# Out-degrees summed by TensorE from the finished rows of counts, in place of a histogram of sources; the capacity check looks at in-degrees alone

## What is computed

```
src = randint(0, 3125)                          # 50000 of them, uniform
dst = int32(3125 * uniform() ** 2.0)            # 50000, skewed to low numbers
order = argsort(dst, stable); src, dst = src[order], dst[order]
deg  = segment_sum(ones, row=src)               # out-degree, layer 0
w    = rsqrt(deg)[src] * rsqrt(deg)[dst]        # where deg > 0
h    = segment_sum(w * x[dst], src) @ W + b     # layer 0
mean = segment_sum(h[src], dst) / max(in_deg,1) # the three mean layers
```

## Time and profile before

| what | value |
|---|---|
| median of 3 runs | 3809.99 us (3808.7 to 3810.3) |
| profiled execution | 3814.58 us, of which span 3812.8 us |
| mean granted clock of TensorE | 0.889 of full |
| DVE busy over the span | 1841.9 us (48%) |
| count_packed, from its first instruction to the first of the stage behind count_pairs | 81.70 to 541.20 us |

### The profile page before, as it was taken

One profiled execution on the slowest core, in us unless ns is written; L12 is line 12 of the kernel. 1 busy time (PEld: TensorE's weight loads), 2 busy tenths in 40 slices (PEclk: granted clock), 3 DMA queues, 4 the chain that ended last, 5 costly groups with the idle time before them and its releaser, 6 DMA issues. The chain is left out here.

```text
span 3812.8 us, 46850 instructions
## 1 busy us (share of the span) xinstructions
PE 2943.8 (77%) x13253; PEld 2097.5 (55%) x13317; DVE 1841.9 (48%) x4590; ACT 875.8 (23%) x1237; POOL 1276.3 (33%) x929
## 2 busy tenths in 40 slices
PE   1777759774666666699999969999998999655565
PEld 1345537643555544466666658989894444344443
DVE  5999852355888887533233323434344221322223
ACT  0135644220100101022222224444441222000000
POOL 2000000007777740177667720000000000477776
PEclk9999979886677678899999989999999999778777
DMA  2046768314444421212222127666861444433334
GB/s 60 18 172 221 270 238 276 113 55 146 129 135 132 128 59 42 78 59 80 80 80 72 68 96 258 199 212 196 276 193 67 142 144 138 124 105 105 105 105 123
DMA packets 325254, 504.89 MB, mean 132 GB/s; under 512 B 27225, under 2 KB 238877, under 8 KB 317005
## 3 DMA queue, kind: packets, MB, share of 16 engines
q1 hardware_dynamic: 284477, 391.28, 30.5%
q0 software_dynamic: 40672, 112.31, 10.6%
HBM read 351.56 MB, written 152.75 MB: 132 GB/s over the span
## 5 line engine op out<-in xcount | busy, mean ns | idle before, releaser
L1791 POOL DMA_INDIRECT e7got<-rel_d,rel_i x416 | 394.6, 948 | 1139.9 <-POOLq L2699 1013.4
L1911 POOL DMA_INDIRECT a_got<-feat_d,src_i x416 | 404.1, 971 | 409.5 <-POOLq L2240 283.0
L1827 PE MATMUL e7sums<-e7got,e7hot 128*128 128x256 f32 x832 | 289.6, 508 | 197.0 <-DMA e7got<-rel_d,rel_i 166.4
L1425 PE MATMUL s_aggs<-s_blk_r,high 128*128 128x512 f32 (+1 forms) x1050 | 400.8, 382 | 20.7 <-DVE low L1544 20.5
L1425 PE MATMUL s_aggs<-s_blk_r,low 128*128 128x512 f32 (+1 forms) x1050 | 389.1, 371 | 0.0
L2740 PE MATMUL q_prods<-w,q_xt 128*128 128x512 f32 x800 | 352.8, 599 | 13.4 <-ACT q_xt L2760 13.4
L1827 PEld LDWEIGHTS e7sums<-e7got,e7hot 128*128 128x128 f32 x832 | 203.0, 255 | 280.4 <-issue 243.2
L1643 POOL TENSOR_SCALAR g_absent<-g_pairs 128x3200 bf16<-128x3200 f32 x25 | 274.8, 10992 | 171.4 <-DMA g_pairs<-pairs_d 171.3
L1690 PE MATMUL g_sums<-value,g_turned 128*128 128x257 f32 x1250 | 299.0, 383 | 8.6 <-ACT g_turned L1754 8.6
L1668 PE MATMUL g_scores<-key_t,g_q 128*128 128x512 f32 (+1 forms) x700 | 280.6, 556 | 19.9 <-DMA g_q<-query_d 13.3
L1799 DVE TENSOR_SCALAR e7hot<-iota,dloc,weight 128x128 f32<-128x128 f32 x416 | 115.7, 364 | 356.6 <-PE e7sums L1827 348.1
(11 more groups left out here) (422 smaller groups left out, 4469.7 us busy)
## 6 DMA issues: line engine op xcount, KB each, us to landing
s_blk<-turned_d SPq DMA_DIRECT2D x60, 1280.0 KB, 5.9
rel_d<-q_rows SPq DMA_DIRECT2D x25, 2048.0 KB, 7.5
s_blk<-turned_d SPq DMA_DIRECT2D x45, 960.0 KB, 5.1
pairs_d<-u_rows SPq DMA_DIRECT2D x25, 1600.0 KB, 8.1
turned_d<-u_line SPq DMA_DIRECT2D x25, 1600.0 KB, 7.1
g_pairs<-pairs_d SPq DMA_DIRECT2D x25, 1600.0 KB, 6.8
t_blk<-pairs_d SPq DMA_DIRECT2D x20, 1280.0 KB, 10.0
t_blk<-pairs_d SPq DMA_DIRECT2D x15, 960.0 KB, 5.1
```

The lines of the kernel that those rows point to most:

```text
L1425: last = pe.matmul(aggs[:, idx % 2, half, 0:w], feats[l][part][:, a, half * P:(half + 1) * P], blk_r[:, q % RINGS, a % GA, 0:w], start=a = ...
L1791: pool.indirect_dma_start(got[:, j % U, :], None, table, bass.IndirectOffsetOnAxis(ap=index[:, j:j + 1], axis=0)).then_inc(arrived[j % U / ...
L1827: return pe.matmul(sums[:, 0:D], hot[:, u, :], got[:, u, :], start=False, stop=False)
L1911: pool.indirect_dma_start(got[:, n % 2, s, :], None, table, bass.IndirectOffsetOnAxis(ap=k.src_i[:, j:j + 1], axis=0)).then_inc(arrived[n ...
```

## The change

The marks and tallies in count_packed go, with hist and its two reductions. TensorE now sums the columns of rows itself. For each of the seven groups of a turn it first multiplies the group (w up to 512 columns of rows, as float32r) by marks[:, g, :], a 128x7 matrix with ones in column g, and accumulates into bank sums, whose row g then holds the out-degrees of group g. The transposes become products with a float32r identity. After the last turn, given gets the 7 x 512 sums, four transposes stand them upright, and two copies bring them to k.deg_src. The check takes **the largest in-degree alone** and compares it with 255.5; the out-degree and the minimum are gone. count_pairs is not edited. The diff, cut to its core (declarations of the names left out):

```diff
...
@@ -750,7 +751,7 @@
                       allow_small_or_imprecise_dtypes=True).then_inc(ready, 1)
             pool.memset(zero[:], 0.0).then_inc(ready, 1)
             pool.memset(hot_s[:, :, THIRD:W], 1.0).then_inc(ready, 1)
-            pool.memset(rows[:], 0.0).then_inc(ready, 1)
+            pool.memset(rows[:].bitcast(F32), 0.0).then_inc(cleared, 1)
 
         @block.vector
         def _(dve):
@@ -761,14 +762,12 @@
             step(dve.scalar_tensor_tensor(column[:], third[:], float(-THIRD), column[:], ALU.mult, ALU.add))
             step(dve.tensor_scalar(value[:], second[:], 255.0, 1.0, ALU.mult, ALU.add))
             step(dve.scalar_tensor_tensor(value[:], third[:], 65280.0, value[:], ALU.mult, ALU.add))
-            dve.wait_ge(ready, 4)
-
-            def marks(i, b):
-                dve.wait_ge(tallied, i + 1)
-                dve.tensor_tensor(marked[:, b, :, 0:P], k.iota_b[0:EP, :].unsqueeze(1).broadcast_to([EP, 4, P]),
-                                  cols(k.slo, i * 4, 4).unsqueeze(2).broadcast_to([EP, 4, P]), ALU.is_equal).then_inc(hot, 1)
-                dve.tensor_tensor(marked[:, b, :, P:P + T], k.iota_b[0:EP, 0:T].unsqueeze(1).broadcast_to([EP, 4, T]),
-                                  cols(k.shi, i * 4, 4).unsqueeze(2).broadcast_to([EP, 4, T]), ALU.is_equal).then_inc(hot, 1)
+            step(dve.tensor_copy(ident_r[:], k.ident[:]))
+            step(dve.tensor_copy(marks[:].rearrange("p g m -> p (g m)"), k.zero[:, 0:1].broadcast_to([P, FLIPS * FLIPS])))
+            step(dve.tensor_copy(marks[:].rearrange("p g m -> p (g m)")[:, 0:FLIPS * FLIPS:FLIPS + 1],
+                                 k.ones[:, 0:FLIPS]))
+            dve.sem_inc(marked, 1)
+            dve.wait_ge(ready, 3)
 
             def take_apart(t):
                 dve.wait_ge(copied, t * COPIES + 2 * COPIES)
@@ -789,10 +788,8 @@
             def eight(i, closing):
                 for u in range(8):
                     j = i * 8 + u
-                    if u % 4 == 0:
-                        if closing:
-                            closings((i * 2 + u // 4 - LOOK))
-                        marks(2 * i + u // 4, u // 4)
+                    if u % 4 == 0 and closing:
+                        closings((i * 2 + u // 4 - LOOK))
                     dve.wait_ge(used, j + 1)
                     dve.tensor_scalar(hot_d[:, u, :], k.iota_b[:], cols(k.dloc, j, 1), None, ALU.is_equal).then_inc(made, 1)
                     dve.tensor_scalar(hot_s[:, u, 0:THIRD], places[:], cols(column, j, 1), cols(value, j, 1),
@@ -804,23 +801,25 @@
             for group in range(S // 4 - LOOK, S // 4):
                 closings(group)
             take_apart(T - 1)
-            dve.wait_ge(final, 1)
-            step(dve.tensor_copy(k.deg_src[:], hist[:, 0:T]))
-            step(dve.tensor_reduce(largest[:, 0:1], k.deg_dst[:], AX.X, ALU.max))
-            step(dve.tensor_reduce(largest[:, 1:2], k.deg_src[:], AX.X, ALU.max))
+
+            step(dve.tensor_reduce(largest[:], k.deg_dst[:], AX.X, ALU.max))
             dve.sem_inc(reduced, 1)
             dve.wait_ge(laid, 1)
-            step(dve.tensor_reduce(flag[:, 0:1], hist[0:1, P:2 * P], AX.X, ALU.max))
-            step(dve.tensor_reduce(flag[:, 1:2], hist[0:1, 2 * P:3 * P], AX.X, ALU.max))
-            step(dve.tensor_tensor(flag[:, 0:1], flag[:, 0:1], flag[:, 1:2], ALU.min))
-            step(dve.tensor_scalar(flag[:, 0:1], flag[:, 0:1], 255.5, None, ALU.is_gt))
-            step(dve.tensor_copy(k.heavy[:], flag[:, 0:1]))
+            step(dve.tensor_reduce(flag[:], counts[0:1, 0, 0:P], AX.X, ALU.max))
+            step(dve.tensor_scalar(flag[:], flag[:], 255.5, None, ALU.is_gt))
+            step(dve.tensor_copy(k.heavy[:], flag[:]))
+            dve.wait_ge(final, 1)
+            step(dve.tensor_copy(given[:], sums[0:FLIPS, :]))
+            dve.sem_inc(given_in, 1)
+            dve.wait_ge(upright, 1)
+            by_group = counts[:, 1, 0:4 * FLIPS].rearrange("p (a g) -> p g a", a=4)
+            step(dve.tensor_copy(k.deg_src[:, 0:4 * (FLIPS - 1)].rearrange("p (g a) -> p g a", a=4), by_group[:, 0:FLIPS - 1, :]))
+            step(dve.tensor_copy(k.deg_src[:, 4 * (FLIPS - 1):T], by_group[:, FLIPS - 1, 0:T - 4 * (FLIPS - 1)]))
 
         @block.tensor
         def _(pe):
             pe.sem_inc(used, RING)
-            pe.sem_inc(tallied, 2)
-            pe.wait_ge(ready, 4)
+            pe.wait_ge(ready, 3)
 
             def zeros(b):
 
@@ -842,24 +841,21 @@
 
             for b in range(BANKS):
                 zeros(b)
-            pe.matmul(hist[:, 0:T], zero[0:EP, 0:P], zero[0:EP, 0:T], start=True, stop=False)
+            pe.matmul(sums[0:FLIPS, :], zero[:, 0:FLIPS], zero[:, 0:512], start=True, stop=False)
+            pe.wait_ge(marked, 1)
 
 
             def flip(closing, g):
                 pe.wait_ge(lined, closing * FLIPS + flip_room(g))
                 pe.sem_inc(k.passed, 1)
+                w = min(4, T - 4 * g) * P
+                pe.matmul(sums[0:FLIPS, 0:w], marks[:, g, :], rows[:, 4 * g * P:4 * g * P + w], start=False, stop=False)
                 for a in range(4 * g, min(T, 4 * g + 4)):
-                    last = pe.transpose(flips[:, g % 4, (a % 4) * P:(a % 4 + 1) * P], rows[:, a * P:(a + 1) * P], k.ident[:])
+                    last = pe.matmul(flips[:, g % 4, (a % 4) * P:(a % 4 + 1) * P], rows[:, a * P:(a + 1) * P], ident_r[:],
+                                     start=True, stop=True)
                 last.then_inc(flipped, 1)
 
-            def tally(i, b):
-                pe.wait_ge(hot, 2 * i + 2)
-                for u in range(4):
-                    last = pe.matmul(hist[:, 0:T], marked[:, b, u, 0:P], marked[:, b, u, P:P + T], start=False, stop=False)
-                last.then_inc(tallied, 1)
-
             def four(i, b):
-                tally(i, b)
                 word = load_word(pe, k, i)
                 with pe.If((word & 15) == 0):
                     for u in range(4):
@@ -887,22 +883,28 @@
             with pe.Fori(0, S // 8) as i:
                 four(2 * i, 0)
                 four(2 * i + 1, 1)
-            pe.matmul(hist[:, 0:T], zero[0:EP, 0:P], zero[0:EP, 0:T], start=False, stop=True).then_inc(final, 1)
             for n in range(BANKS):
                 end(n).then_inc(full, 1)
             for closing in (T - 1, T):
                 pe.wait_ge(spread_out, closing * 3 + 3)
                 for g in range(FLIPS):
                     flip(closing, g)
-            pe.wait_ge(reduced, 1)
-            pe.transpose(hist[0:1, P:2 * P], largest[:, 0:1], k.ident[:])
-            pe.transpose(hist[0:1, 2 * P:3 * P], largest[:, 1:2], k.ident[:]).then_inc(laid, 1)
+                if closing == T - 1:
+                    pe.wait_ge(reduced, 1)
+                    pe.wait_ge(copied, T * COPIES + COPIES)
+                    pe.transpose(counts[0:1, 0, 0:P], largest[:], k.ident[:]).then_inc(laid, 1)
+            pe.matmul(sums[0:FLIPS, :], zero[:, 0:FLIPS], zero[:, 0:512], start=False, stop=True).then_inc(final, 1)
+            pe.wait_ge(given_in, 1)
+            for a in range(4):
+                last = pe.transpose(counts[:, 1, a * FLIPS:(a + 1) * FLIPS], given[:, a * P:(a + 1) * P], k.ident[0:FLIPS, 0:FLIPS])
+            last.then_inc(upright, 1)
 
         @block.scalar
         def _(act):
             act.sem_inc(copied, COPIES)
             act.sem_inc(spread_out, 3)
             act.sem_inc(parted, 3)
+            act.wait_ge(cleared, 1)
             act.sem_inc(lined, FLIPS)
 
             def keep(closing, b):
@@ -946,7 +948,7 @@
             def store(t):
                 sp.wait_ge(spread_out, t * 3 + 6)
                 sp.sem_inc(k.passed, 1)
-                sp.dma_start(pairs_d[bass.ds(t * P, P), :], rows[:]).then_inc(stored, 16)
+                sp.dma_start(pairs_d[bass.ds(t * P, P), :], rows[:].bitcast(F32)).then_inc(stored, 16)
 
             def store_turned(t, b):
                 sp.wait_ge(lined, t * FLIPS + 3 * FLIPS)
```

More of the change, by code:

```diff
@@ L731, in count_packed @@
         apart = sb("apart", [P, 3, THIRD], I32)
-        rows = sb("rows", [P, NP])
+        rows = sb("rows", [P, NP], F32R)
         line = sb("line", [P, 2, NP])
-        largest, flag = sb("largest", [P, 2]), sb("flag", [1, 2])
-        marked = sb("marked", [EP, 2, 4, P + T], BF16)
-        hist = c.enter_context(nc.psum_tensor("u_hist", [P, 512], F32))
+        largest, flag = sb("largest", [P, 1]), sb("flag", [1, 1])
+        ident_r, marks = sb("ident_r", [P, P], F32R), sb("marks", [P, FLIPS, FLIPS], F32R)
+        given = sb("given", [FLIPS, 512])
+        sums = c.enter_context(nc.psum_tensor("u_sums", [P, 512], F32))
         counts = c.enter_context(nc.psum_tensor("u_counts", [P, BANKS, 512], F32))
         flips = c.enter_context(nc.psum_tensor("u_flips", [P, 4, 512], F32))
-        (ready, made, used, hot, tallied, final, full, copied, parted, spread_out, linked, vstep) = (sem(n) for n in (
```

(5 more changed lines are left out.)

## The result

The changed kernel takes 4918.09 us (median, 4909.58 to 4933.75) beside 3809.34 us before: ratio 1.2917 [1.2883, 1.2951], 1109 us slower. The forecast was 4886 us, its range 4785 to 4990. The profiled execution took 4909.58 us, span 4907.8.

A forecast was written before the change was run, and what follows sets the result against it. No engine is full over the span; in the counting stage VectorE paces long tiles, the store's round trip late ones. 3814.6 - 52 + 1128 = 4890.6 us for the profiled execution, 4.6 over the median: 4886 us, range 4785 to 4990.

The forecast's parts named there:

- part 1: In count_packed: marks leave VectorE, TensorE gains the sums; -52 us in all, with ends of -81 and -30.
- 1128 forecast: In count_pairs, run in full: first half 665 us plus second half 463 us, together +1128 us.
- the flag: In the check: largest in-degree 856 exceeds 255.5, so count_pairs runs in full; the rival, flag stays 0, 3758 us, chance 0.03.
- the 32: In count_packed, the twelve tiles after tile 0: 32 us gained of 42 us of removed marks, TensorE being next.
- the 7: In count_packed, the last twelve tiles: they keep the store's pace, for 7 us more gain.
- A bound of +40 for TensorE's lower level: On the total: TensorE's episodes at the lower level could add up to 40 us.
- Slot of count_pairs, 1.54 us: In count_pairs' first half: VectorE's one-hots and marks take 1.54 us a slot, 639 us for 416 slots.
- the 5300 us rival: In count_pairs' first half: the odd 1525-column piece runs at one column per cycle, +415 us, total 5300 us; chance 0.03.
- Who paces the first half: In count_pairs: VectorE paces by little, 1.54 us a slot against TensorE's 1.36; about 10 us of tile-end waits stay.
- Turn, 463 us: In count_pairs' second half: a chain of store, load, transposes and copies, 18.2 us a cycle, 463 us in all.
- the rival of overlap at 4797: In count_pairs' second half: load and store overlap fully, cycle 14.5 us, -89 us, total 4797 us; chance 0.07.
- Held at 1.2 GHz, 5370: In count_pairs' first half: TensorE, held at 1.2 GHz, paces at 2.7 us a slot, +480 us, total 5370; chance 0.04.

The follow-up runs named there:

- e1: The changed kernel with the flag's bound raised from 255.5 to 4095.5, so count_pairs is skipped: 4141.7 us, ratio 0.998 to the kernel before.
- e2: The kernel before with one line removed, so the flag compares the in-degree alone: 5266.35 us, ratio 1.2718 to the kernel before.
- e10: The changed kernel with the smaller of both largest degrees compared again, so count_pairs is skipped: 3811.32 us, ratio 0.9989 to the kernel before.
- e9: The kernel of e10 plus two products by zeros in each group of four slots without a tile's end: 3796.67 us, ratio 0.9958 to the kernel before.
- e6: The changed kernel with the loads of count_pairs' second half issued two tiles ahead: 4726.51 us, ratio 1.2409 to the kernel before.
- e12: The kernel of e9 without the seven sum products of each turn: 3790.45 us, ratio 0.9949 to the kernel before.
- e11: The kernel of e10 with a ring of sixteen one-hot slots in count_packed in place of eight: 4218.03 us, ratio 1.1064 to the kernel before.
- e8: The kernel of e10 with f32 transposes in place of float32r products: 3803.75 us, ratio 0.9973 to the kernel before.

## Why the prediction was right

4886 was forecast and 4918 measured: 32 us, of which part 1 is +48 and count_pairs -15 (1128 forecast; 1109 + 4 by the medians, 1114 between the traces). The two errors have opposite signs, so the total lies nearer than part 1 does by some luck; the mechanism, the flag and a full count_pairs, is the one that was forecast.

- **The flag: right.** e1 and e2 isolate it: 1118 us by one line.
- **Part 1, -52 us: the step that failed**, and outside its bounds too (-78 to -27). e10 has -4 us (-9 to +1). The trace of the changed kernel, at -16, is from the fastest of its four runs, of a stage whose traces spread over 20 us. By the ends of tiles in it (tile 0 at 145.28 us, before 158.34; the twelfth after it at 352.76, before 370.40, and 1.2 us of this lie ahead of the stage), tile 0 gave 12 of the 16 us, the next twelve 5 of the 32, the rest nothing of the 7. What is wrong is the sum of one engine's work as a tile's time. For the tile above, 11 slots, it gives 11 x 0.43 + 2.0 + 1.2 + 1.6 + 1.5 = 11.0 us for TensorE and 8.8 for VectorE, and the tile took 12.4; TensorE idled 2.7 of them, where the sum has 1.5. The turn's price was about right (4.6 us with a slot in it). The twelve tiles behind tile 0 show it at large: by the forecast's terms the longer engine's work is 201 us before and 172 after (a gain of 29, where the text took 32), and they took 212 and 207. What stands above the longer engine's sum (waits of one engine for another, and TensorE's lower level) grew from 11 to 36 us. The last twelve tiles were not bound by VectorE before either: they took 138 us, then 136, where its work is 120 and 97; the 7 us taken for them had no working. A bound of +40 for TensorE's lower level stood in the text, on the total; e10 against e9 puts 12 us of it in this stage, across two chips.
- **Slot of count_pairs, 1.54 us: 1.43.** The one-hots took 626 and 611 ns, not 681 and 663. By starts the pieces of 128, 1525 and 1600 columns are 0.17, 0.53 and 0.54 us, on one line of 0.25 ns a column; on it the 1042 columns of the earlier trace rows would be 0.40, and they are 0.46. They have two operand columns (u_column, u_value) where these have one, which may be the difference; no run isolates it. The odd piece is not slow: the 5300 us rival is out.
- **Who paces the first half: right inside a tile, mis-sized at its ends.** VectorE is full in tile 0 (110.0 of 110 us) and nearly so to 700 us (99.0 of 100). But 44 us fewer of its work (416 x 0.11) are balanced by 48 us of waits for TensorE, where the text let 10 stay, and by 25 us of entry and end (670 - 595 - 48 leaves 27 at most) for 15.5. 665 against 670 is two errors that cancel.
- **Turn, 463 us: 448.** Mean cycle (1629.60 - 1202.54) / 24 = 17.8 us for 18.2, -10 us; from the last store to the next stage 8.0 for 13.1, -5. That load and store add up is confirmed; the rival of overlap at 4797 is out. The rule of the Trainium skill ("DMA: Bandwidth & Descriptors", "Two DMAs through the same engine are not ordered"), reading and writing as separate, pipelined queues, is one of order and names no throughput; the overlap that the text drew from it did not come: 9.5 us by the two rates one after the other, 9.6 in e6.
- **Held at 1.2 GHz, 5370: out.** From 550 to 1150 us the granted clock is 0.98 to 1.00.

What stays open: how much of the 48 us of gain that did not come belongs to the lock-step of TensorE and VectorE. The late tile above shows its waits, e12 leaves little room for TensorE's work alone, but the run made for it (e11) broke on another thing. A rival that no run isolates is the round trip of the store of rows: it released ScalarE's casts in 5 tiles, all late, before (8.2 us of waits) and in 5 after (8.4 us), in 7 in e10 (12.3 us). The forecast read it as the pace of every late tile, and about every second one bears that out.

## What to carry to other kernels

A check that is loosened or tightened by an edit is priced by what it guards: read the values that the data give it before any instruction is counted, since one comparison here outweighs the edit proper, some 1113 us (1109 + 4) against 4. When work goes from the engine that paces a stage, the gain ends where the next engine's waits begin, so draw one tile with both engines in order and not two sums side by side. Before a loop is unrolled further, count the instructions of its body on each engine.

## What the runs showed that was not expected

- Less work on TensorE bought little at once: without the sums, in the profiled executions, the granted clock between 205 and 385 us went from 0.97 to 0.88, with the same busy time (150.2 and 149.8 us) and the same stage (426.6 and 426.5). More work, by zeros, raised it to 1.00, and e9 is 12 us below e10 and 6 below e8 by the ratios.
- The same kernel (e10) took 3788 to 3820 us in twelve runs, where the kernel before, whose VectorE was busy 169 of 180 us in the stretch above, stayed within 8 us in seventeen on the same chip. That a stage without a full engine passes TensorE's levels on to the time is the likely reason, not isolated: on the first chip the kernel before itself spreads over 31 us in 29 runs. One trace of such a stage is a sample.
- A TensorE loop with sixteen slots in its body made the stage 404 us longer in 26 passes, and the cause shows only as "issue" and on the instruction queue.
